# Gated cross-attention with a sign-weight feed-forward: another mask operand, another order of the lead and of the last two groups

## The reference

```python
Q = layernorm(x) @ Wq.T + bq ;  K = ctx @ Wk.T + bk ;  V = ctx
scores = where(mask, -inf, Q @ K.T)          # 128 x 128, one head of width 256, no 1/sqrt(d)
x1 = x + tanh(g_xattn) * (softmax(scores) @ V @ Wo.T + bo)
w = +1 where weights >= 0, else -1
out = x1 + tanh(g_ffn) * clip((layernorm(x1) @ w.T) * scale + bias, -100, 100)
```

## Time and profile before

| | us |
|---|---|
| median of 3 runs | 87.29 (87.25 to 87.45) |
| the profiled execution | 87.51 |
| its span, first to last instruction | 85.8 |
| PE busy | 71.8 (84%) |
| POOL busy | 58.8 (69%) |
| DVE busy | 52.8 (62%) |
| ACT busy | 36.8 (43%) |

### The profile page before, as it was taken

The page is one execution under the profiler, slowest core; times in us unless marked ns, Lnnn a source line. Parts: engine busy times, 40 slices in busy tenths (PEclk is TensorE's granted clock), DMA queues, the critical chain, the costliest instruction groups (busy, mean ns, idle before and its releaser), DMA issues.

```text
span 85.8 us, 1574 instructions
## 1 busy us (share of the span) xinstructions
PE 71.8 (84%) x528; PEld 65.5 (76%) x528; DVE 52.8 (62%) x153; ACT 36.8 (43%) x98; POOL 58.8 (69%) x105
## 2 busy tenths in 40 slices
PE   2999999597799999999999999999999996635000
PEld 2999997495599979979997997999799795414000
DVE  0057764895059849938974980894498187594430
ACT  0142547655629507552950855395085436020000
POOL 5002888934892905889999688999998819568740
PEclk9999999999999999999999999999999999999555
DMA  0899999920000000030003003000300300300303
GB/s 24 253 344 370 349 348 349 348 72 0 0 0 0 0 0 11 0 113 17 0 0 122 8 0 122 0 0 0 122 8 0 122 0 0 110 12 0 122 0 122
DMA packets 7697, 7.44 MB, mean 87 GB/s; under 512 B 775, under 2 KB 7434, under 8 KB 7690
## 3 DMA queue, kind: packets, MB, share of 16 engines
q1 hardware_dynamic: 7360, 7.34, 26.3%
q10 hardware_dynamic: 330, 0.01, 0.2%
HBM read 5.25 MB, written 2.10 MB: 86 GB/s over the span
## 4 chain that ended last, share of the span: by engine, by line
PE 63%; POOL 14%; DVE 8%; issue 5%; DMA 5%; POOLq 1%; ACTq 0%; DVEq 0%
PE ps_K L465 12%; PE ps_Z L465 11%; PE ps_S L526 9%; PE ps_O L545 8%; PE ps_F L465 8%; DMA bk_col<-in_L_xattn_bk_dram 5%; PE ps_xT L460 4%; PE ps_x1T L460 4%; PE ps_cT L460 3%; POOL xn L284 3%; POOL f_biased L302 3%; POOL mask_sel L318 2%; DVE f_scaled L391 2%; PE ps_S L534 2%; PE ps_S L521 2%
## 5 line engine op out<-in xcount | busy, mean ns | idle before, releaser
L302 POOL TENSOR_TENSOR f_biased<-f_scaled,bi_g 128x256 f32<-128x256 f32 x16 | 11.4, 734 | 8.6 <-DVE f_scaled L391 8.6
L383 DVE SCALAR_TENSOR_TENSOR x_sb<-ps_O,recip_p,xb_sb 128x256 f32<-128x256 f32 x16 | 7.0, 479 | 14.1 <-PE ps_O L545 11.9
L186 ACT CAST cT_hi<-ps_cT 128x512 fp32r<-128x512 f32 x8 | 4.7, 585 | 17.9 <-PE ps_cT L460 17.9
L296 POOL TENSOR_TENSOR xb_sb<-x_sb,bo_g 128x256 f32<-128x256 f32 x16 | 11.3, 727 | 0.0
L465 PE MATMUL ps_F<-wT,x1T_hi 128*128 128x256 f32 x32 | 8.7, 304 | 2.3 <-DVE x1T_lo L368 2.3
L284 POOL TENSOR_SCALAR xn<-x_sb,rstd_x,off_x 128x256 f32<-128x256 f32 x16 | 9.9, 624 | 0.5
L465 PE MATMUL ps_Z<-woT_hi,cT_hi 128*128 128x256 f32 x32 | 9.6, 299 | 0.0
L526 PE MATMUL ps_S<-K_sb,xT 128*128 128x128 f32 x64 | 9.3, 288 | 0.0
L465 PE MATMUL ps_K<-cT_hi,wqk_hi 128*128 128x256 f32 x32 | 9.1, 284 | 0.0
L465 PE MATMUL ps_K<-cT_hi,wqk_lo 128*128 128x256 f32 x32 | 9.0, 282 | 0.0
L465 PE MATMUL ps_K<-cT_lo,wqk_hi 128*128 128x256 f32 x32 | 9.0, 281 | 0.0
(11 more groups left out here) (94 smaller groups left out, 193.5 us busy)
## 6 DMA issues: line engine op xcount, KB each, us to landing
ctx_sb<-in_ctx_dram SPq DMA_DIRECT2D x8, 256.0 KB, 6.5
x_sb<-in_x_dram SPq DMA_DIRECT2D x8, 256.0 KB, 6.3
out_dram<-out_sb SPq DMA_DIRECT2D x8, 256.0 KB, 2.1
wq_sb<-in_L_xattn_Wq_dram SPq DMA_DIRECT2D x1, 256.0 KB, 3.0
wk_sb<-in_L_xattn_Wk_dram SPq DMA_DIRECT2D x1, 256.0 KB, 3.8
wo_sb<-in_L_xattn_Wo_dram SPq DMA_DIRECT2D x1, 256.0 KB, 4.8
w_sb<-in_L_ffn_weights_dram SPq DMA_DIRECT2D x1, 256.0 KB, 5.6
bq_col<-in_L_xattn_bq_dram ACTq DMA_DIRECT2D x1, 1.0 KB, 3.2
```

Of the source, the lines that this page charges most:

```text
L296: nc.gpsimd.tensor_tensor(xb_sb[:, r], x_sb[:, r], bo_g[:], ALU.add).then_inc(xb_done, 1)
L302: nc.gpsimd.tensor_tensor(f_biased[:, r], f_scaled[:, r], bi_g[:], ALU.add).then_inc(f_biased_done, 1)
L383: nc.vector.scalar_tensor_tensor(out=x1_sb[:, r], in0=ps_O[:, b], scalar=recip_p[:, r:r + 1], in1=xb_sb[:, r], op0=ALU.mult, op1=ALU.add). ...
```

## The change

- **Mask.** `mask_sel` (one operand for each group) and the ones matrix go. There is one mask operand, `mask_blk`, 128 rows by 258 columns, for all groups, and the group is picked by a constant 128 x 128 selector `sel[:, g]` as the stationary side. GpSimd only fills it; VectorE makes the selectors from the identity ahead of Wq and scales the mask bytes into it.
- **Lead.** 20 transposes of the identity and not 24; x(0) is loaded ahead of ctx(0), x(1) ahead of Wo, the mask ahead of the gates; VectorE begins Wq without waiting for bk; the folded weights come ahead of ctx(0)'s transposes, `transpose_x(0)` stands inside `project_K(0)`, Wo's transposes behind it; the scale is spread into another bank, in stage 0 behind the transposes of `w_cent`.
- **The last two groups.** The loops end a stage earlier and the rest is written out. scores(7) comes ahead of attend(6); rstd_1s(7) ahead of bias_and_clip(6); group 6's last addition is GpSimd's; group 7's bias, clip and last addition are VectorE's, row by row, each row with its own store.

The diff, without declarations, renamed semaphores, and the loops' bounds (`G - 1` in place of `G + 1` or `G + 2`, with the conditions that this makes needless):

```diff
-WARM_UP = 24
+WARM_UP = 20
...
-        mask_row = sb("mask_row", [B, GB, K1], BF16)
-        mask_sel = sb("mask_sel", [B, G, GB, K1], BF16)
-        ones_b = sb("ones_b", [B, P], BF16)
+
+        mask_blk = sb("mask_blk", [P, GB, K1], BF16)
+        place, group_of = sb("place", [P, GB]), sb("group_of", [P, G])
...
             sp.dma_start(wk_sb[:], wk.rearrange("(p c) d -> p c d", c=DC)).then_inc(wk_loaded, 16)
+            load_x(0)
             load_ctx(0)
-            load_x(0)
+            load_x(1)
             sp.dma_start(wo_sb[:], wo.rearrange("(c p) d -> p c d", p=P)).then_inc(wo_loaded, 16)
-            load_x(1)
...
+            sp.wait_ge(out_p_done, GB)
+            sp.dma_start(out_rows[:, rows(G - 2), :], out_sb[:, rows(G - 2), :]).then_inc(stored, 16)
+            for b in range(GB):
+                r = (G - 1) * GB + b
+                sp.wait_ge(out_last_done, b + 1)
+                sp.dma_start(out_rows[:, r, :], out_sb[:, r, :]).then_inc(stored, 16)
+            sp.wait_ge(stored, 16 * (G + 1))
...
-            act.dma_start(bq_col[:], bq.rearrange("(p c) -> p c", c=DC)).then_inc(bqk_loaded, 16)
+            act.dma_start(bq_col[:], bq.rearrange("(p c) -> p c", c=DC)).then_inc(bq_loaded, 16)
+            act.dma_start(bk_col[:], bk.rearrange("(p c) -> p c", c=DC)).then_inc(bk_loaded, 16)
+            act.dma_start(mask_u8[:], mask).then_inc(mask_loaded, 16)
-            act.dma_start(mask_u8[:], mask).then_inc(mask_loaded, 16)
...
-            evict_cT_hi(0)
...
+            evict_cT_hi(0)
...
+            evict_xT(0)
+            evict_K(0)
             act.wait_ge(tanh_ready, 1)
             act.wait_ge(ps_woT_ready, 1)
             nc.scalar.activation(woT_hi[:], ps_woT, ACT.Identity, scale=tanh_g[:, 0:1]).then_inc(woT_hi_ready, 1)
-            evict_K(0)
-            evict_xT(0)
-            act.wait_ge(ps_rows_ready, 1)
+            act.wait_ge(ps_bo_ready, 1)
...
-                    nc.scalar.activation(sc_g[:], x1T_bank[:, D:2 * D], ACT.Identity, scale=tanh_g[:, 1:2]
-                                         ).then_inc(sc_g_ready, 1)
-                    act.wait_ge(ps_bi_ready, 1)
-                    nc.scalar.activation(bi_g[:], f_bank[:, 0:D], ACT.Identity, scale=tanh_g[:, 1:2]).then_inc(bi_g_ready, 1)
                     act.wait_ge(ps_wT_ready, 1)
                     nc.scalar.copy(wT[:], ps_x1T).then_inc(wT_ready, 1)
+                    act.wait_ge(ps_rows_ready, 1)
+                    nc.scalar.activation(sc_g[:], f_bank[:, 0:D], ACT.Identity, scale=tanh_g[:, 1:2]).then_inc(sc_g_ready, 1)
+                    nc.scalar.activation(bi_g[:], f_bank[:, D:2 * D], ACT.Identity, scale=tanh_g[:, 1:2]
+                                         ).then_inc(bi_g_ready, 1)
+            exp(G - 1)
+            evict_Z(G - 1)
+            evict_PT(G - 1)
+            evict_x1T_hi(G - 2)
+            evict_x1T_hi(G - 1)
...
-            nc.gpsimd.memset(mask_row[:], FLOOR).then_inc(mask_filled, 1)
+            nc.gpsimd.memset(mask_blk[:], 0.0).then_inc(mask_filled, 1)
+            pool.wait_ge(mask_filled, 1)
+
+            nc.gpsimd.memset(mask_blk[:, 0, P:P + 1], FLOOR / GB).then_inc(mask_filled, 1)
+            nc.gpsimd.memset(mask_blk[:, 1, 0:1], FLOOR / GB).then_inc(mask_filled, 1)
...
-            pool.wait_ge(mask_loaded, 16)
-            pool.wait_ge(mask_filled, 1)
-            for b in range(GB):
-                nc.gpsimd.tensor_scalar(mask_row[:, b, b:b + P], mask_u8[:], MASKED, 1.0, ALU.mult, ALU.mult
-                                        ).then_inc(mask_filled, 1)
-            pool.wait_ge(mask_filled, 1 + GB)
-            nc.gpsimd.affine_select(out=mask_sel[:], in_=mask_row[:, :, :].rearrange("p (o b) k -> p o b k", o=1).to_broadcast([B, G, GB, K1]),
-                                    compare_op=ALU.is_equal, fill=0.0, base=0, pattern=[[-GB, G], [-1, GB], [0, K1]],
-                                    channel_multiplier=1).then_inc(mask_ready, 1)
...
+            rstd_1s(G - 1)
+            bias_and_clip(G - 2)
+            for b in range(GB):
+                r = (G - 2) * GB + b
+                pool.wait_ge(f_clip_done, G - 1)
+                nc.gpsimd.tensor_tensor(out_sb[:, r], f_clip[:, (G - 2) % 2, b], x1_sb[:, r], ALU.add).then_inc(out_p_done, 1)
...
+            def last_group():
+                dve.wait_ge(rstd_1_done, G)
+                dve.wait_ge(F_prod, G)
+                for b in range(GB):
+                    r = (G - 1) * GB + b
+                    nc.vector.scalar_tensor_tensor(out=f_scaled[:, r], in0=ps_F[:, b], scalar=rstd_1[:, r:r + 1],
+                                                   in1=sc_g[:], op0=ALU.mult, op1=ALU.mult).then_inc(f_scaled_done, 1)
+                    dve.wait_ge(f_scaled_done, r + 1)
+                    nc.vector.tensor_tensor(f_biased[:, r], f_scaled[:, r], bi_g[:], ALU.add).then_inc(f_last_done, 1)
+                    dve.wait_ge(f_last_done, 2 * b + 1)
+                    nc.vector.tensor_scalar(f_last[:, b], f_biased[:, r], clip_hi[:, 0:1], clip_lo[:, 0:1], ALU.min, ALU.max
+                                            ).then_inc(f_last_done, 1)
+                    dve.wait_ge(f_last_done, 2 * b + 2)
+                    nc.vector.tensor_tensor(out_sb[:, r], f_last[:, b], x1_sb[:, r], ALU.add).then_inc(out_last_done, 1)
+
+            dve.wait_ge(ident_ready, 1)
+            nc.vector.tensor_reduce(place[:], ident[:].rearrange("p (g b) -> p b g", b=GB), AX.X, ALU.add).then_inc(place_done, 1)
+            nc.vector.tensor_reduce(group_of[:], ident[:, 0:B].rearrange("p (g b) -> p g b", b=GB), AX.X, ALU.add
+                                    ).then_inc(group_of_done, 1)
+            dve.wait_ge(group_of_done, 1)
+            nc.vector.tensor_scalar(sel[:], group_of[:, :].rearrange("p (g o) -> p g o", o=1).to_broadcast([P, G, P]),
+                                    1.0, None, ALU.mult).then_inc(sel_done, 1)
...
+            split_wqk(0)
+            dve.wait_ge(place_done, 1)
+            dve.wait_ge(mask_filled, 3)
+            dve.wait_ge(mask_loaded, 16)
+            for b in range(GB):
+                nc.vector.tensor_scalar(mask_blk[0:B, b, b:b + P], mask_u8[:], MASKED, place[0:B, b:b + 1], ALU.mult, ALU.mult
+                                        ).then_inc(mask_ready, 1)
+            split_wqk(1)
             split_cT(0)
...
+            scale_ffn_out(G - 3)
+            max_of_scores(G - 1)
+            residual(G - 2)
+            stats_x1(G - 2)
+            final(G - 3)
+            split_x1T(G - 2)
+            residual(G - 1)
+            stats_x1(G - 1)
+            split_x1T(G - 1)
+            scale_ffn_out(G - 2)
+            last_group()
...
+                    if between and m == 0:
+                        between()
...
+                    pe.wait_ge(sel_done, 1)
+                    pe.wait_ge(mask_ready, GB)
+                nc.tensor.matmul(ps_S_both, sel[:, g], mask_blk[:, :, :].rearrange("p b k -> p (b k)"), start=True, stop=False)
...
-            transpose_ctx(0)
             pe.wait_ge(wk_loaded, 16)
             pe.wait_ge(wq2_ready, DC)
             for m in range(DC):
                 accumulate(ps_wqk[m], [(wk_sb[:, e, m * P:(m + 1) * P], wq2[:, e]) for e in range(DC)]
                            ).then_inc(ps_wqk_ready, 1)
-            pe.wait_ge(bqk_loaded, 32)
+            transpose_ctx(0)
+            pe.wait_ge(bk_loaded, 16)
...
+            project_K(0, between=lambda: transpose_x(0))
             pe.wait_ge(wo_loaded, 16)
             transposes(ps_woT, wo_sb).then_inc(ps_woT_ready, 1)
-            project_K(0)
-            transpose_x(0)
             pe.wait_ge(rows_loaded, 48)
-            nc.tensor.matmul(x1T_bank[:, 0:D], ones_1[:], bo_row[:], start=True, stop=True)
-            nc.tensor.matmul(x1T_bank[:, D:2 * D], ones_1[:], sc_row[:], start=True, stop=True).then_inc(ps_rows_ready, 1)
...
                 if i == 0:
-                    pe.wait_ge(woT_lo_ready, 1)
-                    nc.tensor.matmul(f_bank[:, 0:D], ones_1[:], bi_row[:], start=True, stop=True).then_inc(ps_bi_ready, 1)
                     pe.wait_ge(bo_g_ready, 1)
-                    pe.wait_ge(sc_g_ready, 1)
                     pe.wait_ge(w_cent_ready, DC)
                     transposes(ps_x1T, w_cent).then_inc(ps_wT_ready, 1)
+                    pe.wait_ge(woT_lo_ready, 1)
+                    nc.tensor.matmul(f_bank[:, 0:D], ones_1[:], sc_row[:], start=True, stop=True)
+                    nc.tensor.matmul(f_bank[:, D:2 * D], ones_1[:], bi_row[:], start=True, stop=True).then_inc(ps_rows_ready, 1)
                 else:
...
+                if i == G - 2:
+                    scores(G - 1)
+                attend(i)
+            project_Z(G - 1)
+            transpose_p(G - 1)
+            transpose_x1(G - 2)
+            attend(G - 1)
+            ffn(G - 2)
+            transpose_x1(G - 1)
+            ffn(G - 1)
```

(80 more changed lines are left out.)

32 lines of the change are left out of this document (17 added, 15 removed).

## The result

The changed kernel takes 83.56 us (83.25 to 83.95, 4 runs) against 87.27 (87.05 to 87.45) in the same measurement, a ratio of 0.956 (0.952 to 0.960): 3.7 us faster. Run once more beside the other kernels it was 83.66, 0.960 (0.956 to 0.964).

The account below looks back on a forecast made before the run. TensorE was taken to bound the loop (five unchanged 7.47 us stages), with waits outside it and VectorE and GpSimd at the end. 87.51 - 1.4 (lead) - 1.1 (end) = 85.0, less 0.22 gives 84.8; range 83.6 to 86.2.

Parts of the forecast that it names:

- The mask matmul: In each of 8 groups: 128 rows cost as much as 16, change 0; ends 0.14 cost or 0.05 gain each.
- The sign that I had named: In the loop: a stage that is not 7.47 us would show the prediction wrong.
- The lead: From the start to attend(0): 1.4 us gained, 0.64 up to K(1) and 0.76 behind it.
- K(1)'s start: In the lead: K(1) starts at 17.5 to 18.1, not 18.39, a gain of 0.3 to 0.9; 0.64 taken.
- The part behind K(1): From K(1) to attend(0), 4.01 before: the wait in stage 0 goes, net gain 0.76, ends 0.3 and 1.0.
- The end: Last two groups: 1.1 us gained, 0.9 plus 0.2 for the store, with ends 0.6 and 2.4.
- holding by GpSimd: Group 7's eight VectorE operations: unheld they end at 81.8, fully held at 82.6; 82.3 taken.
- The last store: At the end: 128 KB and not 256, a gain of 0.2, between 0 and 1.0.
- The clock: In the lead: TensorE's clock assumed to rise at the same time as before, about 7.25 us.
- The late rise: Rival: TensorE's clock rises late in the lead; at 14 it gives 89; 0.06, with anything else turning the sign.
- my first rival: At the end: the clock falls before ffn(7) as TensorE stands still 2.4 us; 0.5 to 0.95 more, 85.5; chance 0.14.
- The third rival: Both port holding and gates are absent: lead 1.9, end 1.8, giving 83.6; chance 0.10.

Follow-up runs that it names:

- the lead alone: The changed kernel with the old order of the last two groups and a mask matmul of 16 rows: 85.37 us, 0.978 of the kernel before.
- the new end alone: The kernel before with only the new order of the last two groups, group 7 on VectorE and its two stores: 86.75 us, 0.993.
- the old end: The changed kernel, keeping its lead and 128-row mask, with the last two groups in the order of before: 83.55 us, 0.958.
- group 6's additions last: The changed kernel with group 6's last additions moved from GpSimd to VectorE, behind group 7, their store last: 83.69 us.
- lead and end both new: The changed kernel with its mask matmul reading only 16 rows: 84.82 us, 0.972 of the kernel before.
- the wait for bk: The changed kernel with VectorE again waiting for bk before it sums Wq: 84.20 us, 0.964 of the kernel before.
- the old scale: The changed kernel with the feed-forward scale again spread in the lead, so TensorE waits for ScalarE's copy in stage 0: 84.41 us, 0.964.
- 128-row spreads: The changed kernel with its three one-row parameter-spreading matmuls reading 128 rows, 127 of them zeros: 82.84 us, 0.953 of the kernel before.

## Why the prediction was wrong, step by step

- **The mask matmul: the step that failed.** It said "Rows don't set the time" and took 0, with 0.05 of gain for each group as its end on that side. For the matmul itself that is true. The 0.27 a group lies between it and its neighbours, and it stood in the profile: a weight load with 0.33 of idle time before it, in each stage. The sign that I had named, a stage other than 7.47, came: 7.19. I had read the loop's windows, where TensorE is busy without a gap, and so never asked what was between its instructions. The runs with 16, 64 and 96 rows show 1.0 to 1.2 us, that with 128 rows on the old kernel 1.6; the traces, 1.65 and 1.86.
- **The lead: the mechanism right, mis-sized.** 1.4 was forecast (0.6 to 1.9), 2.0 measured by the lead alone. With 0.07 added, to put them on the old axis: Wq at 3.91 (3.79 forecast), K(0) at 9.9 (10.35), scores at 13.1 (13.35), K(1) at 17.1 (17.5 to 18.1), attend(0) at 20.4 (20.8 to 21.3). The term that was off is K(1)'s start: 1.3 sooner, where I took 0.64. VectorE's maxima began at 14.9 and not at 15.3 to 15.9. Some 0.4 of that is that the whole chain from K(0) on came sooner, so that the subtraction for Wo ended at 14.3 and not at 14.75; and the absolute value took 0.31 and not up to 0.87. The part behind K(1) is 3.34 in place of 4.01, so 0.67, near the 0.76 forecast.
- **The end: mis-sized, and partly not there.** ffn(7) started where the order put it: 16.47 us behind stage 6's mask matmul by the forecast, 16.42 with 16 rows. From its start to the last addition I had 5.1; with 16 rows it took 5.6 (75.41 to 81.01). Of that, holding by GpSimd is 0.68, where I took 0.5 of the 0.8 that I had as its upper end; I had counted only operations with two SBUF inputs, but the clip was held too. ffn(7) to its result took 1.3 and not 1.1, and the eight operations less the holding 3.6 and not 3.5. So the compute part is 0.5 (22.02 against 22.50 from stage 6's mask matmul) and not 0.9. The last store gave 0.4 rather than 0.2. But the time outside the span, 1.7 before, is 2.1 to 2.2 in the runs of the changed kernel. It is 1.8 with the new end alone or the old end, 1.8 to 1.9 with group 6's additions last, but also 1.8 with lead and end both new and the wait for bk: some 0.35 is lost where the trace shows nothing. Why stays open. With the stop of group 7, hidden by the new end, it is why the parts don't add.
- **The clock.** I took one time for the rise. In fact the first folded-weight loads take 190 ns at 5.4 in one execution and 333 at 5.6 to 6.7 in another of the same lead, and stage 1's mask matmul comes at 20.85 or at 21.98. So where the clock rises moves the new lead's end by 1.1 us from run to run. The late rise, the rival that would have turned the sign, didn't happen. A fall before ffn(7), my first rival, didn't happen in the profiled execution, where ffn(7) takes 1.20. But in the profile of the repeated run the granted clock falls within it, after 2.3 us in which TensorE stood still (1.00 in the window 72:73, 0.64 in 73:74, 0.50 in 74:75):

```profile
72.96 1.78 PE ps_F L514 x8
```

From stage 1's mask matmul to the last addition that execution takes 57.99 in place of 57.70: half of the 0.58 that ffn(7) loses is won back behind it, as the rival had it, since GpSimd's additions are done before row 0's last one, which takes 0.42 and not 0.82. It took 1.93 in the profile of the run with the old scale and 1.48 in that with 128-row spreads, so this rival is a part of the spread of the small effects above.

The forecasts without the mask are borne out: 84.8 was forecast, and the changed kernel with 16 rows takes 84.82. That is partly luck, since the lead was 0.6 too small and the end as much too large. The third rival's 83.6 is luck altogether: it is the measured time, but it left out the holding, which was there, and had nothing for the mask.

## What to carry to other kernels

Look at the weight loads beside every matmul whose contraction has 64 rows or fewer among matmuls of 128: a repeated idle time put down to "issue" is the price of the change, and rows of zeros take it away. A busy engine is not one without gaps; before writing that a stage is bound and can't change, list the idle time between its instructions. Price work that VectorE and GpSimd do side by side on SBUF with the holding in it (here 0.68 of two operations' 0.84), for operations with one SBUF input too, and test the parts of a change together as well as alone.

## What the runs showed of the hardware

- The stop of a matmul of 16 or 64 rows among those of 128 rows is 0.33 us before its weight load; with 96 or 128 rows it is none. A group loses 0.27 net.
- A tensor_scalar with per-partition clip bounds, one SBUF input, took 0.70 beside a GpSimd addition and 0.41 without; I had expected only operations with two inputs to be held.
- The rise and the fall of TensorE's clock lie at different places in executions of one kernel: its weight loads of the folded weights took 190 ns in one and up to 333 in the other, and its ffn(7) 1.78 and 1.20 us.
